# Layer 0 of a four-layer kernel: one written order of steps for front and feed-forward, weight pieces multiplied by VectorE

## What is computed

```python
q, k, v = x @ Wq + bq, x @ Wk + bk, x @ Wv + bv     # x normalised; q (16, 32 heads), k and v 16 wide
o = softmax(q * k / 4) * v                          # 16 x 16 scores per token, summed over e
x = x + layernorm(o broadcast over the 32 heads)
W_eff = W * (su @ sv)                               # su: 4 columns, sv: 4 rows; for gate, up and down
x = x + layernorm((silu(h @ gate_eff.T) * (h @ up_eff.T)) @ down_eff.T)    # h = layernorm(x), 1792 wide inside
```

## Time and profile before

| | |
|---|---|
| median of 3 runs | 4261.45 us (4254.96 to 4264.74) |
| span of the profiled execution, first to last instruction | 4243.4 us |
| its own time as a run | not given; the median is 18.05 us above the span |
| busy share of the span: PE, DVE, ACT, POOL | 89%, 66%, 54%, 45% |
| front, 0 to 187.7 us | PE busy 127.9 us, DVE 125.4 us |
| feed-forward part, 190.3 to 630.3 us | PE busy 440.0 us, DVE 132.5 us |

### The profile page before, as it was taken

How to read it: one execution, slowest core, us unless ns; L and a number is a source line. 1 busy time by engine, 2 the same in 40 slices (tenths; PEclk the granted TensorE clock), 3 DMA queues, 4 the chain that set the end, 5 groups by cost and what they waited for, 6 DMA issues and landing times.

```text
span 4243.4 us, 63398 instructions
## 1 busy us (share of the span) xinstructions
PE 3775.5 (89%) x21648; PEld 1876.8 (44%) x21648; DVE 2793.0 (66%) x4541; ACT 2277.0 (54%) x3947; POOL 1888.5 (45%) x1566
## 2 busy tenths in 40 slices
PE   6799998899888779999999999999999985867899
PEld 2344443223322245555555555555555542443344
DVE  6633235774675468888888888988888866566322
ACT  5522223555456556676666667666676644453222
POOL 5500000000000347787786878777787774462000
PEclk9999997889889989999999999999999997998999
DMA  3100001001100010000000000000000010012100
GB/s 110 54 6 1 0 12 34 1 1 18 35 7 4 10 42 1 24 12 25 13 14 24 1 25 13 25 13 19 18 1 27 4 37 27 23 46 73 31 10 20
DMA packets 62821, 91.36 MB, mean 22 GB/s; under 512 B 12357, under 2 KB 36440, under 8 KB 62500
## 3 DMA queue, kind: packets, MB, share of 16 engines
q1 hardware_dynamic: 61832, 86.72, 7.2%
q10 hardware_dynamic: 672, 0.59, 0.1%
HBM read 73.62 MB, written 6.85 MB: 19 GB/s over the span
## 4 chain that ended last, share of the span: by engine, by line
PE 65%; DVE 15%; issue 8%; ACT 6%; POOL 4%; DMA 1%; SPq 1%; DVEq 0%; POOLq 0%; ACTq 0%
PE psum L329 14%; PE psum L330 14%; PE psum L331 14%; PE psum L1396 3%; DVE arena L1558 3%; PE psum L2499 2%; PE psum L2503 2%; PE psum L1369 2%; PE psum L2491 2%; PE psum L2460 2%; PE psum L1380 2%; ACT xn L218 1%; DVE x L2185 1%; PE psum L2482 1%; PE psum L1365 1%
## 5 line engine op out<-in xcount | busy, mean ns | idle before, releaser
L329 PE MATMUL psum<-xt_hi,arena 128*128 128x512 f16 (+2 forms) x2272 | 872.7, 384 | 31.4 <-DVE arena L531 10.8
L330 PE MATMUL psum<-xt_lo,arena 128*128 128x512 f16 (+2 forms) x2272 | 872.0, 384 | 0.0
L331 PE MATMUL psum<-xt_hi,arena 128*128 128x512 f16 (+2 forms) x2272 | 871.0, 383 | 0.0
L2286 POOL TENSOR_TENSOR arena<-arena 128x1024 f16<-128x1024 f16 x256 | 514.5, 2029 | 50.3 <-DVE arena L2097 33.5
L1314 POOL TENSOR_TENSOR rs<-sd,epsc 128x1 f32<-128x1 f32 x15 | 8.2, 548 | 1087.5 <-DVE sd L1606 1087.5
L329 PE MATMUL psum<-arena 128*128 128x512 f16 (+1 forms) x1152 | 422.4, 370 | 58.3 <-DVE arena L2914 19.0
L1509 ACT ACTIVATE arena<-psum 128x512 f32<-128x512 f32 x576 | 319.7, 598 | 266.3 <-PE psum L1380 176.7
L1558 DVE TENSOR_REDUCE arena<-psum 128x1 f32<-128x512 f32 (+3 forms) x608 | 365.1, 654 | 148.1 <-PE psum L1369 147.1
L330 PE MATMUL psum<-arena 128*128 128x512 f16 (+1 forms) x1152 | 422.2, 370 | 0.0
L331 PE MATMUL psum<-arena 128*128 128x512 f16 (+1 forms) x1152 | 422.1, 370 | 0.0
L329 PEld LDWEIGHTS psum<-xt_hi,arena 128*128 128x128 f16 (+1 forms) x2272 | 224.6, 99 | 280.9 <-issue 16.0
(11 more groups left out here) (338 smaller groups left out, 7882.1 us busy)
## 6 DMA issues: line engine op xcount, KB each, us to landing
arena<-m_wi SPq DMA_DIRECT2D x64, 320.0 KB, 3.0
arena<-m_wo SPq DMA_DIRECT2D x32, 256.0 KB, 2.6
arena<-arena SPq DMA_DIRECT2D x90, 64.0 KB, 2.5
x<-L_attn_x SPq DMA_DIRECT2D x4, 1024.0 KB, 8.3
out<-x SPq DMA_DIRECT2D x4, 1024.0 KB, 4.3
arena<-gate_wT SPq DMA_DIRECT2D x16, 224.0 KB, 2.5
arena<-up_wT SPq DMA_DIRECT2D x16, 224.0 KB, 2.5
arena<-down_wT SPq DMA_DIRECT2D x14, 256.0 KB, 2.6
```

Source lines behind the costliest of these rows:

```text
L329: nc.tensor.matmul(out, lh, rh, start=start, stop=False)
L330: nc.tensor.matmul(out, lh, rl, start=False, stop=False)
L331: return nc.tensor.matmul(out, ll, rh, start=False, stop=stop)
L2286: nc.gpsimd.tensor_tensor(m4_ar[:, q], heads[q].broadcast_to([P, HG, P]), m4_le.unsqueeze(1).broadcast_to([P, HG, P]), ALU.mult).then_inc( ...
```

## The change

Layer 0 becomes one list of steps that all five queues follow, front and feed-forward together.
- Ahead of everything the factors of all three weights are loaded (18 loads, high and low copies stacked to 76 rows) and brought to float16 by ScalarE and VectorE, so that the factor matmul is one float16 matmul.
- A piece is multiplied by VectorE, reading the factor product from PSUM and writing over the raw piece. ScalarE's copy and GpSimd's multiply are gone. There are three raw buffers, and a load waits for GpSimd's subtraction of the piece three before.
- Pieces are ordered so that the first eight serve blocks 0 to 2 of gate and up. Sixteen piece steps stand ahead of the first block, two follow each block of group 0, the rest stands after block 13.
- The first gate block follows the attention and the turned tiles of group 0. Attention and turned tiles of groups 1 to 3 stand between the blocks of the group before (input tiles: two groups before). From the ninth entry on all turns use one bank.
- Statistics of four tiles share one power -0.5 on GpSimd in place of Sqrt and reciprocal. Layer 1's first weights move from group 0 to group 1. All groups are written out.

The step list, the loads, and the core of each queue:

```diff
+        RAW1 = 3
+        raw1 = carve(SCR + 8192, [RAW1, C], F32)
+        FR = 76
+        fac_w = carve(86016, [FW], F32)
+        fac_n = carve(93184, [3, C], F32)
+        fac_wh = carve(133120, [FW], F16)
+        fac_nh = carve(FRONT + 11776, [3, C], F16)
...
-        for m, (h_, l_) in enumerate(((gh, gl), (uh, ul))):
+        for c in range(4):
             for k in range(KT):
-                for c in range(4):
+                for m, (h_, l_) in enumerate(((gh, gl), (uh, ul))):
                     chunks.append((m, k, slice(c * QW, (c + 1) * QW), h_[:, k, c * QW:(c + 1) * QW],
                                    l_[:, k, c * QW:(c + 1) * QW]))
         for f in range(F0):
             chunks.append((2, f, slice(0, C), dh[:, f, :], dl[:, f, :]))
-        first_of = {0: 0, 1: 16, 2: 32}
...
+        SEQ0 = []
+        for kind, g in (("x0", 0), ("x0", 1), ("ln", 0), ("x0", 2), ("ln", 1), ("tail", 0), ("x0", 3), ("ln", 2), ("tail", 1),
+                        ("ln", 3), ("tail", 2), ("tail", 3)):
+            SEQ0 += [(kind, g * GT + j) for j in range(GT)]
+        BATCH0 = [n for n in range(0, len(SEQ0), GT) if SEQ0[n][0] != "tail"]
...
+        def bank0(n):
+            return 6 + n % 2 if n < 2 * GT else 6
...
+        def steps0():
+            steps, made = [], 0
+            def chunk(n=1):
+                nonlocal made
+                for _ in range(n):
+                    if made <= len(chunks):
+                        steps.append(("chunk", made))
+                        made += 1
+            def planes(n):
+                return [("tr", n), ("hi", n), ("lo", n)]
+            n = entry0("x0", 0)
+            steps.append(("factors", 0))
+            steps += [("stat", n + j) for j in range(GT)] + [("var", n)]
+            chunk(2)
+            steps += [("scale", n), ("norm", n), ("norm", n + 1)]
+            for j in range(GT):
+                steps += planes(n + j)
+                if j + 2 < GT:
+                    steps.append(("norm", n + j + 2))
+                chunk()
+            m = entry0("x0", GT)
+            steps.append(("qkv", 0))
+            steps += [("stat", m), ("stat", m + 1)]
+            chunk(2)
+            steps += [("logits", 0), ("stat", m + 2), ("stat", m + 3), ("var", m), ("maxima", 0), ("scale", m), ("weights", 0)]
+            chunk(2)
+            steps += [("norm", m), ("norm", m + 1), *planes(m), ("means", 0)]
+            chunk(2)
+            steps += [("norm", m + 2), *planes(m + 1), ("add", 0)]
+            chunk()
+            n = entry0("ln", 0)
+            steps += [("stat", n + j) for j in range(GT)] + [("var", n)]
+            chunk()
+            steps += [("norm", m + 3), *planes(m + 2), *planes(m + 3), ("scale", n), ("norm", n), ("norm", n + 1)]
+            for j in range(GT):
+                steps += planes(n + j)
+                if j + 2 < GT:
+                    steps.append(("norm", n + j + 2))
+                if j % 2:
+                    chunk()
+            for g in range(NG):
+                before, after = {}, {}
+                add = lambda where, f, *what: where.setdefault(f, []).extend(what)
+                def batch(n, f):
+                    add(after, f, *[("stat", n + j) for j in range(GT)], ("var", n))
+                    add(after, f + 1, ("scale", n), ("norm", n), ("norm", n + 1))
+                    for j in range(GT):
+                        add(before, f + 2 + j, ("tr", n + j))
+                        add(after, f + 2 + j, ("hi", n + j), ("lo", n + j))
+                        if j + 2 < GT:
+                            add(after, f + 2 + j, ("norm", n + j + 2))
+                if g + 1 < NG:
+                    add(after, 1, ("qkv", g + 1))
+                    for q, part in enumerate(ATTN0[1:]):
+                        add(after, 2 + q, (part, g + 1))
+                    batch(entry0("ln", (g + 1) * GT), 8)
+                if g + 2 < NG:
+                    batch(entry0("x0", (g + 2) * GT), 2)
+                for f in range(F0):
+                    steps.append(("gate", g, f))
+                    if g and f == 1:
+                        steps.append(("carry", g - 1))
+                    steps.extend(before.get(f, []))
+                    steps.append(("up", g, f))
+                    chunk(2)
+                    steps.extend(after.get(f, []))
+                steps.append(("hidden", g))
+                chunk(len(chunks))
+                steps += [("tile", g, j) for j in range(GT)]
+            return steps
...
+        def sp_l0(sp):
+            load_x(sp, 0)
+            sp.wait_ge(w1_made, 2)
+            for m, (wide, narrow) in enumerate((("gate_suT", "gate_sv"), ("up_suT", "up_sv"), ("down_sv", "down_suT"))):
+                for part in range(3):
+                    rows = slice(32 * part + RANK * m, 32 * part + RANK * (m + 1))
+                    sp.dma_start(fac_w[rows, :], A[wide]).then_inc(w1_fac, 16)
+                    sp.dma_start(fac_n[rows, m, :], A[narrow]).then_inc(w1_fac, 16)
             for i, (m, k, cols, _, _) in enumerate(chunks):
-                if i == first_of[m]:
-                    if m:
-                        sp.wait_ge(w1_ps, i)
-                    wn, fr, fc = names[m]
-                    if m == 1:
-                        sp.dma_start(suT[0:RANK, :], A[fr]).then_inc(w1_fac, 16)
-                        sp.dma_start(svT[0:RANK, :], A[fc]).then_inc(w1_fac, 16)
-                    elif m == 2:
-                        sp.dma_start(suT[0:RANK, :], A["down_sv"]).then_inc(w1_fac, 16)
-                        sp.dma_start(svT[0:RANK, :], A["down_suT"]).then_inc(w1_fac, 16)
-                if i >= 2:
-                    sp.wait_ge(w1_eff, i - 1)
+                if i == 2:
+                    sp_l0_attn(sp)
+                if i in (4, 10, 16):
+                    load_x(sp, 1 + (i - 4) // 6)
+                if i >= RAW1:
+                    sp.wait_ge(w1_lo, i - RAW1 + 1)
                 w = cols.stop - cols.start
-                sp.dma_start(raw1[:, i % 2, 0:w], A[wn][k * P:(k + 1) * P, cols]).then_inc(w1_raw[i % 2], 16)
+                name = ("gate_wT", "up_wT", "down_wT")[m]
+                sp.dma_start(raw1[:, i % RAW1, 0:w], A[name][k * P:(k + 1) * P, cols]).then_inc(w1_raw[i % RAW1], 16)
...
-        def pool_l0_ffn(pool):
-            for i in range(len(chunks) + 1):
-                if i < len(chunks):
-                    w = chunks[i][2].stop - chunks[i][2].start
-                    pool.wait_ge(w1_rk, i + 1)
-                    pool.wait_ge(w1_raw[i % 2], 16 * (i // 2 + 1))
-                    if i >= 2:
-                        pool.wait_ge(w1_lo, i - 1)
-                    nc.gpsimd.tensor_tensor(we1[:, i % 2, 0:w], rank1[:, i % 2, 0:w], raw1[:, i % 2, 0:w],
-                                            ALU.mult).then_inc(w1_eff, 1)
-                if i:
-                    m, k, cols, h_, l_ = chunks[i - 1]
-                    w = cols.stop - cols.start
-                    pool.wait_ge(w1_hi, i)
-                    nc.gpsimd.tensor_tensor(l_, we1[:, (i - 1) % 2, 0:w], h_, ALU.subtract).then_inc(w1_lo, 1)
-        def pe_front(pe):
+        def pool_l0(pool):
+            for what, n, *f in STEPS0:
+                if what == "var":
+                    b = BATCH0.index(n)
+                    if b >= 2:
+                        pool.wait_ge(x_norm, BATCH0[b - 2] + GT)
+                    pool.wait_ge(x_mv, n + GT)
+                    nc.gpsimd.tensor_tensor(rs0[:, b % 2, 0, :], sd0[:, b % 2, :], epsc[:, 4:5].broadcast_to([P, GT]),
+                                            ALU.pow).then_inc(x_sd, GT)
+                elif what == "means":
+                    pool.wait_ge(a0_var, 2 * n + 1)
+                    nc.gpsimd.tensor_tensor(sc0[:, 2, :], sc0[:, 1, :], epsc[:, 4:5].broadcast_to([P, GT]),
+                                            ALU.pow).then_inc(a0_var, 1)
+                elif what == "chunk":
+                    if n:
+                        m, k, cols, h_, l_ = chunks[n - 1]
+                        w = cols.stop - cols.start
+                        pool.wait_ge(w1_hi, n)
+                        nc.gpsimd.tensor_tensor(l_, raw1[:, (n - 1) % RAW1, 0:w], h_, ALU.subtract).then_inc(w1_lo, 1)
...
-                        pe.wait_ge(xt_ok, n - 1)
+                        pe.wait_ge(xt_ok, n - 1 if n < 2 * GT else n)
...
+                elif what in ("gate", "up"):
+                    pe_l0_block(pe, what, n, *f)
+                elif what == "carry":
+                    Tail.pe_x(pe, entry0("tail", n * GT + GT - 1), GT - 1)
+                elif what == "tile":
+                    g, j = n, f[0]
+                    r = g * GT + j
+                    if r >= 2:
+                        pe.wait_ge(y_norm, r - 1)
...
+                            if g == 0:
+                                if f == 0:
+                                    pe.wait_ge(w1_eff, len(chunks))
```

(58 more changed lines are left out.)

293 lines of the change are left out of this document (148 added, 145 removed).

## The result

Over 20 runs of each kernel the median fell from 4258.2 us (4239.7 to 4270.4) to 4236.98 us (4223.1 to 4255.2). The ratio is 0.995, 95% interval 0.9937 to 0.9963: 21.2 us faster, where 15.5 were forecast. The profiled execution of the changed kernel has a span of 4230.8 us and a time of 4232.61 us; the time of every run with a span on record is the span and 1.8 us.

A forecast was written before the change was run, and what follows sets the result against it. Layer 0 was bound by a front of five queues waiting for each other, then by TensorE alone. First gate matmul 100.4 us earlier, less 84.9 of longer matmul part, gains 15.5: 4246 us, range 4208 to 4276.

The forecast's parts named there:

- The front: Walk along VectorE's queue before the first gate matmul: 22.5 + 48.9 + 15.9 = 87.3 us, 100.4 earlier than before.
- TensorE's own work: Work moved into the matmul part: 30 factor matmuls 5.7 us, 20 turns 12.0, qkv of three groups 6.0; together 23.7.
- The pauses: Group 0: the second piece's factor matmul waits for VectorE's multiply of the first, 1.9 us in 14 blocks, 26.6.
- Attention and turns in group 0: Block 3's product 1.1 us late, turns waiting for low parts behind attention steps 0.65, 0.65, none, 3.0; sum 5.4.
- The last pieces: After block 13, piece 45's load waits for GpSimd's subtraction of piece 42; first y tile waits 5.3 us.
- Group 1: Without pieces, block 3's product is 2.8 us late and turns wait behind normalise and attention steps; sum 14.9.
- The clock: Matmul part: granted clock 0.95 in group 0 costs 5 us, slow matmuls after three long pauses 4; together 9.
- The pauses hidden: Rival: waits and clock loss in the matmul part vanish, only TensorE's 23.7 us remain, time 4185; chance 0.14.
- Pieces holding the front up: Rival: eight piece pairs each wait 3 us on VectorE's queue, first gate matmul at 110, time 4269; chance 0.12.
- The low level for all of group 0: Rival: clock falls to 1.2 GHz through group 0, costing 71 us in place of 5, time 4312; chance 0.09.
- VectorE the bound: Rival: VectorE's 46 multiplies make it group 0's bound, ten stretched instructions cost 10 us more, 4256; chance 0.05.
- The table change: ScalarE's table load priced at 1.28 us; at the skill's 2.66, block 3's product 2.8 later in groups 0 and 1, 4251.

The follow-up runs named there:

- e1_apart: Changed kernel with one piece step behind the gate block and one behind the up block in group 0, instead of two behind up; median 4214.65 us, ratio 0.9894.
- e2_turn_first: Changed kernel with the attention step behind the turned tile's low part from block 3 of each group on, piece steps still paired; median 4220.44 us, ratio 0.9909.
- e3_both: Changed kernel with piece steps apart and attention steps behind the turned tiles, multiply left on VectorE; median 4194.08 us, ratio 0.9852.

## Why the prediction was right

The sign, the mechanism and the shares were as forecast; the time lies 9 us below the 4246 and inside the range. 3.3 of the 9 us come from the base: the difference was taken off the median of three runs, 4261.45, and 20 runs have 4258.2. By the prediction's own steps:

**The front.** The first statistics started at 22.55 us (22.5 forecast; the terms given for it add up to 22.8) and the first gate matmul at 87.70 (87.3). That the second came out so close is luck, as two errors of 5 us cancel in it. VectorE worked for 43.9 us in the walk, not 48.9: the four adds of group 0, priced at 4.7 us, took 2.50. And it stood still for 21.3 us, not 15.9. Its waits for turned copies are one row of the new kernel, 22 to 87.7 us:
```profile
DVE xt_lo L1319 <- ACT xt_hi L1240: 15.7, 8, 2.7
```
That row alone is as long as all the waits that I summed. The serial four tiles at the end were near the forecast, 2.6 us each where 2.44 follow from it: turns at 77.40, 80.02, 82.61 and 85.20. The multiply was priced at 0.6 us. All 46 lie between 0.603 and 0.692, median 0.618:
```profile
L1331 DVE SCALAR_TENSOR_TENSOR arena<-psum,arena x46: 603/618/692, 26.5 to 212.2; 128x448 f32<-128x448 f32 x32, 128x512 f32<-128x512 f32 x14
```

**The length of the part**, 76.7 us more where 84.9 were forecast:
1. TensorE's own work, 23.7 forecast, measured 18.5. A turn among running matmuls occupies 0.44 us (607.03 to 607.47), not 0.60, so 20 are 8.8; qkv 1.22 (104.15 to 105.37), not 2.0, so three are 3.7; a factor matmul 0.20. This is the largest error: I read durations, and starts, where the engine was not yet in flow.
2. The pauses, 26.6 forecast, 25.7 measured in 15 waits, two of them (1.77 and 0.21) behind block 13. e1_apart took 19.8 us of them out and got 22.6 us of time.
3. Attention and turns in group 0, 5.4 forecast, 3.1 measured.
4. The last pieces, 5.3 forecast, 4.1 measured.
5. Group 1, 14.9 forecast, 10.3 measured: turn waits of 4.37, 2.37, 0.33, 2.79 and 0.47 in place of 5.1, 3.1, 1.0, 4.9 and 0.8. The place and cause were right (e2_turn_first), the size was 4.6 too large.
6. Groups 2 and 3, nothing: from 330 to 607 us TensorE is busy for 276.88 of 277.00.
7. The clock, 9 forecast, about 11.0 measured: summed from the timelines, the 512-column matmuls cost 10.6 us more than in before, the turns 0.4. The forecast 0.95 for group 0 is the row's 0.95. Of the slow matmuls behind long pauses, two spells behind turn waits in group 1 are 3.4 us.

These are 72.7 of the 76.7. The 4.0 left are a matter of how a wait is counted. In brackets it counts from the end of the matmul ahead of it, 0.35 to 0.41 us after that one's start (101.87 + 0.35 + 1.73 is 103.95), while in the stream the next starts after 0.20 to 0.23; over 24 waits that makes 4.0 us. The prediction counted its pauses from TensorE's last issue, and counted so the usual one is the 1.9 us forecast, and term 2 is some 28.2, 1.6 too small. Terms 1, 3, 4 and 5, counted so, were 11.8 too large together, 7 was 2.0 too small: part of the errors cancel.

So 23.3 us were gained by the end of layer 0 in place of 15.5, and 21.2 of them in the median.

**The rivals.** The pauses hidden: no, by the 25.7 us. That most of them could be hidden is shown by e3_both, at 4194; the prediction took them to be in the order itself, and so they are: two moved steps take most of them out. Pieces holding the front up: no, VectorE waited 0.3 us for a piece's load in the whole front (2.5 were in my sum). The low level for all of group 0: no, 0.95. VectorE the bound: no, it was busy for 61.3 of 125.3 us in group 0, and e1_apart shortened the part with the same work on it.

**The table change.** The rows priced it at 1.28 us. ScalarE's timeline of the new kernel agrees:
```profile
116.59 1.28 ACT L1260 ACT_TABLE_LOAD   x1
117.89 0.60 ACT L1260 ACTIVATE arena<-psum 128x512 f32<-128x512 f32 x1
```
Silu starts 1.30 us after the load's start. The Trainium skill, "ScalarE: Activation LUTs", section "What ACT_TABLE_LOAD costs", would put 2.66 there; no gap is to be seen here, ahead of the load or behind it, so the measurement decides for the rows' price. The time alone could not have told 4251 from 4246.

**The clock rule.** The granted clock of group 0 was 0.95 with a pause of 1.7 to 1.8 us behind most blocks. The Trainium skill, "TensorE: Matmul & The Clock Gate", section "A second HAM failure mode: psum-queue depth-cycling", describes a clock that swings in such a pattern. It did so for single spells of some 3 us (matmuls 0.43 us apart from 191.0 to 194.4, for one), and not for the group.

## What to carry to other kernels

When independent work is threaded into a full matmul stream, look at what stands ahead of the instruction that frees its buffer in the other engine's queue. Two pieces placed back to back with two banks cost 1.7 us nearly each time, 25.7 in all, though VectorE was half idle. One piece behind each half block cost 5.9 in all, and a copy on an engine whose steps lie half a block earlier 3.6. Price an operation in a stream by the distance between starts in a stream, and judge a kernel's lead by medians: two profiled executions of one kernel here were 11 us apart (4230.8 and 4242.0).

## What the hardware showed that I had not expected

- A wait of TensorE can be paid for again behind it. In group 1 of the new kernel matmuls started 0.43 us apart for 3.4 us each behind turn waits of 4.37 and 2.37 us, but not behind one of 2.79; from 225 to 330 us the granted clock was 0.97, and 1.00 in e2_turn_first without these waits. That run removed 10.7 us of waits and 17.8 us of layer 0.
- The same program gave 4223 to 4255 us in 20 runs, with a mean granted clock of 0.944 or 0.945 in the four runs up to 4225.4 us and 0.937 at 4255.
- GpSimd's power over 128x4 took 1.01 us in the median of eight (one took 1.86), not the 0.55 of the 128x1 form in the earlier trace rows; three of them lay in the front, and VectorE waited 0.2 us for them.
- VectorE's adds slow down beside GpSimd. In the front of the new kernel four adds of 128x512 took 2.50 us while GpSimd stood still. The same four took 4.27 in the kernel before, where GpSimd multiplied and subtracted beside them and two of the four lasted over 1.5 us each.
